# Wb's last four row tiles: 32x32 blocks from the load and a VectorE transpose, in place of TensorE transposes

## The reference

```
x = x + ffn0(cond0(x))     x = x + ffn1(cond1(x))
cond0: x W0^T + 2 * sum over the top-2 of 8 experts of gate * B0 (A0 x), gates from x Wr0 and a bias per language id
ffn0:  top-1 of 8 experts by logits, logit * Bw (A x)
cond1: x W1^T + b1 + 2 * (x As[slot]) Bs[slot], slot per batch element
ffn1:  x Wb^T + b_base + 2 * sum over the top-2 of 8 experts of weight * B1 (A1 x)
```

## Time and profile before

| | |
|---|---|
| median of three runs | 500.59 us |
| the profiled execution, device time | 501.62 us |
| its span, first to last instruction | 499.6 us |
| mean granted TensorE clock | 0.989 |
| TensorE busy / VectorE / ScalarE | 98% / 54% / 27% of the span |

### The profile page before, as it was taken

The page is one execution under the profiler, slowest core; times in us unless marked ns, Lnnn a source line. Parts: engine busy times, 40 slices in busy tenths (PEclk is TensorE's granted clock), DMA queues, the critical chain, the costliest instruction groups (busy, mean ns, idle before and its releaser), DMA issues.

```text
span 499.6 us, 8465 instructions
## 1 busy us (share of the span) xinstructions
PE 487.5 (98%) x3007; PEld 466.5 (93%) x3007; DVE 267.6 (54%) x825; ACT 135.9 (27%) x300; POOL 9.5 (2%) x18
## 2 busy tenths in 40 slices
PE   6999999999999988999999999999999999999997
PEld 4988899999999878999999999999999999999997
DVE  3745864544446746475465574656557457445211
ACT  4444630111111331232132232132124123212111
POOL 2040000000000000000000000000000000000000
PEclk9987999999999999999999999999999999999999
DMA  8975525221111145107304312611710910200111
GB/s 258 331 253 178 183 72 139 106 63 43 42 42 48 44 62 78 54 4 120 71 5 95 53 46 64 83 42 60 89 42 2 148 44 2 64 31 16 59 42 43
DMA packets 86621, 40.22 MB, mean 81 GB/s; under 512 B 68503, under 2 KB 80545, under 8 KB 86462
## 3 DMA queue, kind: packets, MB, share of 16 engines
q1 hardware_dynamic: 86318, 39.25, 31.3%
q0 software_dynamic: 272, 0.56, 0.5%
HBM read 28.64 MB, written 11.16 MB: 80 GB/s over the span
## 4 chain that ended last, share of the span: by engine, by line
PE 96%; DVE 2%; DMA 1%; ACT 1%; issue 0%; DVEq 0%; ACTq 0%
PE banks L1054 28%; PE banks L1056 28%; PE banks L1055 28%; PE banks L1049 5%; PE banks L1068 3%; PE banks L1239 2%; PE banks L1103 1%; DMA a0f<-in_L_ffn_A_dram 1%; PE banks L1077 0%; PE banks L1201 0%; PE banks L1244 0%; DVE xTlo L705 0%; DVE x_raw L752 0%; PE banks L1249 0%; DVE a0f L741 0%
## 5 line engine op out<-in xcount | busy, mean ns | idle before, releaser
L1054 PE MATMUL banks<-Mhi,x1Thi 128*128 128x392 f32 x384 | 137.0, 357 | 2.0 <-DVE x1Tlo L705 1.5
L1055 PE MATMUL banks<-Mlo,x1Thi 128*128 128x392 f32 x384 | 130.6, 340 | 0.0
L1056 PE MATMUL banks<-Mhi,x1Tlo 128*128 128x392 f32 x384 | 130.5, 340 | 0.0
L1054 PEld LDWEIGHTS banks<-Mhi,x1Thi 128*128 128x128 f32 x384 | 72.3, 188 | 4.5 <-issue 2.4
L1054 PE MATMUL banks<-WbThi,ws_hi 128*128 128x392 f32 (+2 forms) x216 | 74.7, 346 | 0.0
L1056 PE MATMUL banks<-WbThi,ws_lo 128*128 128x392 f32 (+2 forms) x216 | 73.2, 339 | 0.0
L1055 PE MATMUL banks<-WbTlo,ws_hi 128*128 128x392 f32 (+2 forms) x216 | 73.0, 338 | 0.0
L1055 PEld LDWEIGHTS banks<-Mlo,x1Thi 128*128 128x128 f32 x384 | 72.5, 189 | 0.0
L1056 PEld LDWEIGHTS banks<-Mhi,x1Tlo 128*128 128x128 f32 x384 | 72.2, 188 | 0.0
L1056 PEld LDWEIGHTS banks<-WbThi,ws_lo 128*128 128x128 f32 x216 | 40.7, 188 | 3.2
L1055 PEld LDWEIGHTS banks<-WbTlo,ws_hi 128*128 128x128 f32 x216 | 40.6, 188 | 3.1
(11 more groups left out here) (180 smaller groups left out, 772.8 us busy)
## 6 DMA issues: line engine op xcount, KB each, us to landing
wraw<-in_L_cond_W_dram SPq DMA_DIRECT2D x16, 512.0 KB, 3.9
out_dram<-ybuf SPq DMA_DIRECT2D x15, 512.0 KB, 3.1
x_raw<-in_x_dram SPq DMA_DIRECT2D x56, 128.0 KB, 3.9
wraw<-in_L_ffn_W_base_dram SPq DMA_DIRECT2D x8, 512.0 KB, 6.5
xin_first<-in_x_dram SPq DMA_DIRECT2D x1, 1024.0 KB, 9.5
x1T_dram<-xin_first SPq DMA_DIRECT2D x1, 1024.0 KB, 3.9
wraw<-x1T_dram SPq DMA_DIRECT2D x2, 512.0 KB, 3.5
Fbuf<-fe_hi_dram SPq DMA_DIRECT2D x16, 64.0 KB
```

Of the source, the lines that this page charges most:

```text
L1054: pe.matmul(out_, l[0], r[0], start=start, stop=False, **kw)
L1055: pe.matmul(out_, l[0], r[1], start=False, stop=False, **kw)
L1056: return pe.matmul(out_, l[1], r[0], start=False, stop=stop, **kw)
```

## The change

Wb tiles 0 to 3 are handled as before. Tiles 4 to 7 are loaded by `load_blocks`, four DMAs each, turned in place by one VectorE transpose (`turn_wb`), and split by one ScalarE copy and one VectorE subtraction of 128x1024 (`wb_part` on both) straight from the `wraw` buffer. Their eight units go. New semaphores: `wb_in` (a tile has landed), `wb_turned_in` (VectorE has turned it), `wb_hi`, `wb_lo` (its parts are there). ScalarE's and VectorE's orders are rewritten, TensorE's fe steps stand alone, and TensorE waits for wb_lo 2 before fe step 8 and for wb_lo 4 before fe step 16. The W1 loads wait for `wb_lo` in place of the units. The counts that wait for W1's and later loads fall by one load for each buffer.

```diff
@@ SyncE
-                sp.dma_start(wraw[o % 4][:, :], Wb[o * P:(o + 1) * P, :]).then_inc(wraw_in[o % 4], 16)
+                if o < 4:
+                    sp.dma_start(wraw[o][:, :], Wb[o * P:(o + 1) * P, :]).then_inc(wraw_in[o], 16)
+                else:
+                    load_blocks(wraw[o - 4], Wb, o, wb_in[o - 4])
...
             for n in range(4):
-                sp.wait_ge(unit_done, wb_turned(4 + n))
+                sp.wait_ge(wb_lo, n + 1)
                 load_w1(n, n)
@@ helper
+        def wb_parts(o):
+            raw = wraw[o - 4][:, :].rearrange("p (k c) -> p k c", k=K)
+            return [(raw, [t[:, :, RC + o * P:RC + (o + 1) * P] for t in (WbThi, WbTlo)])]
@@ ScalarE
-            copy_units(NEF, units_second[NEF - NU1:NEF - NU1 + 4])
+            def wb_part(o):
+                act.wait_ge(wb_turned_in, o - 3)
+                for raw, (hi, _) in wb_parts(o):
+                    ins = act.activation(hi, raw, ACT.Copy)
+                ins.then_inc(wb_hi, 1)
+
+            copy_units(NEF, units_second[NEF - NU1:NEF - NU1 + 2])
+            wb_part(4)
             hgT_part(0)
-            copy_units(NEF + 4, units_second[NEF - NU1 + 4:NEF - NU1 + 8])
+            wb_part(5)
             keep_fe(0)
-            copy_units(NEF + 8, units_second[NEF - NU1 + 8:NEF - NU1 + 10])
+            wb_part(6)
+            wb_part(7)
             xT_part(1, 1, xT_first, XT_FIRST[1])
             whT_part(0, 0)
-            copy_units(NEF + 10, units_bw)
+            copy_units(NEF + 2, units_bw)
@@ VectorE
-            lo_units(NEF, units_second[NEF - NU1:NEF - NU1 + 4])
+            def turn_wb(o):
+                dve.wait_ge(wb_in[o - 4], 64)
+                tile = wraw[o - 4][:, :]
+                dve.transpose(tile, tile).then_inc(wb_turned_in, 1)
+
+            def wb_part(o):
+                dve.wait_ge(wb_hi, o - 3)
+                for raw, (hi, low) in wb_parts(o):
+                    ins = lo(low, raw, hi)
+                ins.then_inc(wb_lo, 1)
+
+            lo_units(NEF, units_second[NEF - NU1:NEF - NU1 + 2])
+            turn_wb(4)
             hgT_part(0)
-            lo_units(NEF + 4, units_second[NEF - NU1 + 4:NEF - NU1 + 8])
+            turn_wb(5)
+            wb_part(4)
             keep_fe(0)
             top1(0)
-            lo_units(NEF + 8, units_second[NEF - NU1 + 8:NEF - NU1 + 10])
+            turn_wb(6)
+            wb_part(5)
+            turn_wb(7)
+            wb_part(6)
+            wb_part(7)
             xT_part(1, 1, xT_first, XT_FIRST[1])
             whT_part(0, 0)
-            lo_units(NEF + 10, units_bw)
+            lo_units(NEF + 2, units_bw)
@@ TensorE
-            for n, unit in enumerate(units_second[NEF - NU1:NEF - NU1 + 10]):
-                if n == 4:
-                    turn_small(hg_ready, 1, pt_hg, hg[:, :], thg_done)
-                if n == 8:
-                    add_lora0(0)
+            for n, unit in enumerate(units_second[NEF - NU1:NEF - NU1 + 2]):
                 turn_units(NEF + n, [unit])
-                if n == 8:
-                    pe.wait_ge(unit_lo, wb_turned(5))
                 fe_steps(n, n + 1)
+            fe_steps(2, 6)
+            turn_small(hg_ready, 1, pt_hg, hg[:, :], thg_done)
+            fe_steps(6, 8)
+            add_lora0(0)
+            pe.wait_ge(wb_lo, 2)
+            fe_steps(8, 10)
             pe.wait_ge(fe_lo, 1)
             turn_x(xin_first[:, D:2 * D], XT_FIRST[1])
             turn_small(wh_ready, 1, pt_wh, wh[:, :], twh_done)
-            turn_units(NEF + 10, units_bw)
+            turn_units(NEF + 2, units_bw)
             fe_steps(10, 12)
             small0(1, 1, xT_first)
             fe_steps(12, 2 * K)
             pe.wait_ge(unit_lo, NU2)
+            pe.wait_ge(wb_lo, 4)
             fe_steps(2 * K, 18)
```

More of the change, by code:

```diff
@@ L161, in adaln_ffn @@
         w1_hi, w1_lo = sem("w1_hi"), sem("w1_lo")
+        wb_in, wb_turned_in = [sem(f"wb_in{i}") for i in range(4)], sem("wb_turned_in")
+        wb_hi, wb_lo = sem("wb_hi"), sem("wb_lo")
         m_done, m_hi, m_lo = sem("m_done"), sem("m_hi"), sem("m_lo")
@@ L223, in adaln_ffn @@
         units_bw = turn_b(bw_j, BwThi, BwTlo, 1.0, [(bw_j_ready, 1)])
-        units_b1 = turn_b(wraw[2], B1Thi, B1Tlo, 2.0, [(wraw_in[2], 16 * 8)])
+        units_b1 = turn_b(wraw[2], B1Thi, B1Tlo, 2.0, [(wraw_in[2], 16 * 7)])
         units_wb = []
-        for o in range(K):
+        for o in range(4):
             for k0 in (0, 4):
@@ L286, in half_tiles, with block_rows @@
             return t[:, :].rearrange("p (k c) -> p k c", k=K)[:, 4 * h:4 * h + 4, half * P:(half + 1) * P]
-        def block_rows(t):
-            return xf[bass.ds(t * P, P), :].rearrange("(i r) (k j c) -> j r k i c", r=BLK, j=NJ, c=BLK)
+        def block_rows(src, t):
+            return src[bass.ds(t * P, P), :].rearrange("(i r) (k j c) -> j r k i c", r=BLK, j=NJ, c=BLK)
         def raw_tile(raw, half, h=None):
@@ L312, in _, with load_blocks @@
             w0v = W0.rearrange("(p j) i -> p j i", j=K)
-            def load_blocks(tile, t, s):
-                src = block_rows(t)
+            def load_blocks(tile, rows_of, t, s):
+                src = block_rows(rows_of, t)
                 for j in range(NJ):
@@ L370, in _ @@
             sp.wait_ge(fe_stored, 32)
-            load_blocks(x_raw1[:, 0:D], 2, x2_in)
+            load_blocks(x_raw1[:, 0:D], xf, 2, x2_in)
             sp.wait_ge(acc_step, 1)
@@ L401, in load_x @@
             def load_x(t, half, raw):
-                load_blocks(raw[:, half * D:(half + 1) * D], t, x_in[half])
+                load_blocks(raw[:, half * D:(half + 1) * D], xf, t, x_in[half])
             sp.wait_ge(w1_hi, K - 1)
@@ L594, in _ @@
             exp0(0)
-            copy_units(NEF, units_second[NEF - NU1:NEF - NU1 + 4])
+            def wb_part(o):
[5 more added lines that the diff above has]
+            wb_part(4)
             hgT_part(0)
-            copy_units(NEF + 4, units_second[NEF - NU1 + 4:NEF - NU1 + 8])
+            wb_part(5)
             keep_fe(0)
-            copy_units(NEF + 8, units_second[NEF - NU1 + 8:NEF - NU1 + 10])
+            wb_part(6)
+            wb_part(7)
             xT_part(1, 1, xT_first, XT_FIRST[1])
             whT_part(0, 0)
-            copy_units(NEF + 10, units_bw)
+            copy_units(NEF + 2, units_bw)
             exp0(1)
-            act.wait_ge(wraw_in[0], 80)
+            act.wait_ge(wraw_in[0], 64)
             act.activation(ws_hi[0][:, :], wraw[0][:, :], ACT.Copy).then_inc(w1_hi, 1)
@@ L608, in _ @@
             keep_fe(2)
-            act.wait_ge(wraw_in[1], 80)
+            act.wait_ge(wraw_in[1], 64)
             act.activation(ws_hi[1][:, :], wraw[1][:, :], ACT.Copy).then_inc(w1_hi, 1)
@@ L629, in _ @@
                     keep_m(i, par)
-                    act.wait_ge(wraw_in[2 + par], i * 16 + 16 * 5)
+                    act.wait_ge(wraw_in[2 + par], i * 16 + 16 * 4)
                     act.activation(ws_hi[par][:, :], wraw[2 + par][:, :], ACT.Copy).then_inc(w1_hi, 1)
@@ L646, in _ @@
                 if g == 0:
-                    act.wait_ge(wraw_in[2], 16 * 9)
-                    act.wait_ge(wraw_in[3], 16 * 8)
+                    act.wait_ge(wraw_in[2], 16 * 8)
+                    act.wait_ge(wraw_in[3], 16 * 7)
                 x1T_part(0, 0, g, sums(g))
```

## The result

The changed kernel takes 507.13 us, the median of six runs (505.29 to 512.26), against 501.12 us, the median of six of the kernel before (500.29 to 504.64). The ratio over all these runs is 1.0129, with a 95% interval of 1.0070 to 1.0188; the two medians alone give 1.0120, which lies inside it. The forecast was 506.9 us, slower. The execution that was profiled after is a long one, 511.0 us on the device, of which the span is 509.2 us; so stretches are compared here, and not whole spans.

The account below looks back on a forecast made before the run. TensorE, holding 96% of the chain of waits, was taken as the bound. A 4.3 us later small0 plus 2.0 us of lowered clock made 6.3 us, taking the median from 500.59 to 506.9 us, range 504.2 to 509.0.

Parts of the forecast that it names:

- The bound: TensorE holds 96% of the chain of waits, with no later slack to swallow a delay made in the changed stretch.
- What is removed: Eight units of transposes on TensorE, 3.5 us, and a 0.40 us wait: 3.9 us of path if nothing else is late.
- The first wait: TensorE before add_lora0(0), waiting 1.5 us for hgT_lo because ScalarE copies tile 4 ahead of its hgT half.
- The second wait: TensorE before fe step 8, idle 6.8 us for wb_lo 2, as tile 5's subtraction follows tile 6's transpose on VectorE.
- The shift of small0: Second small0 starts 4.3 us later, at 68.58 and not 64.31, and the shift lasts to the kernel's end.
- the bounds 2.5 to 5.2: Limits in us on the 4.3 us shift: VectorE's chain without two idle stretches, or every hand-over at 0.14 us.
- The clock: TensorE's clock falls to 1.2 GHz through the 6.8 us idle, costing 1.0 to 2.7 us behind it, 2.0 taken.
- the slow stretch: Low-clock time behind the idle, taken as 2.1 to 5.5 us like earlier rows; at most half of it lost.
- The loads: Block DMAs of tiles 4 to 7 cost nothing; tile 5 has 5 us to spare and more.
- Sum: Whole kernel: 4.3 us of shift plus 2.0 us of clock, 6.3 us slower, median 506.9 us.
- The clock that holds: Rival: the same wait at TensorE but no fall of the clock, 504.9 us; chance 14%.
- The rival on the other side: Rival: tiles come in time, wb_lo 2 by 57.1, and TensorE keeps its 3.9 us, 496.7 us; chance 4%.

Follow-up runs that it names:

- e4: Changed kernel, VectorE and ScalarE reordered: tiles 4 and 5 turned before the first gates, last two subtractions behind the Bw units; 499.60 us, ratio 0.9976 to before.
- e6: e4 with the subtractions of tiles 6 and 7 moved from VectorE to GpSimd; 498.72 us, ratio 0.9965 to the kernel before.
- e2: Changed kernel with twelve dead fe steps (36 matmuls) on TensorE between add_lora0 and the wait for wb_lo 2; 505.20 us, ratio 1.0082 to before.
- e1: Changed kernel run again with no edit; 507.05 us, ratio 1.0125 to the kernel before.
- e5: Changed kernel with VectorE's subtraction of tile 5 moved ahead of keep_fe(0), top1(0) and the transpose of tile 6; 505.02 us, ratio 1.0072 to before.
- e10: e6 repeated with no edit; 499.38 us, ratio 0.9988 to the kernel before.
- e12: e6 with VectorE's transpose of tile 5 moved behind the first gates; 499.63 us, ratio 0.9970 to the kernel before.
- e3: Changed kernel with tiles 4 to 7 loaded by one DMA each in 4 KB rows, output wrong; 507.61 us, ratio 1.0130 to before.
- e8: Kernel before with only the block loads of tiles 4 to 7 added, TensorE's transposes kept, output wrong; 501.04 us, ratio 0.9996 to before.
- e7: Half the change: only tiles 6 and 7 in blocks on VectorE, 4 and 5 left to TensorE's transposes; 501.21 us, ratio 1.0005 to before.
- e9: e6 with tile 4's subtraction on GpSimd too, three in all; 501.91 us, ratio 1.0032 to the kernel before.
- e11: e6 with tiles 4 to 7 loaded by one DMA each in 4 KB rows, output wrong; 498.46 us, ratio 0.9954 to before.

## Why the prediction was right, step by step

- **The bound.** That TensorE has no slack behind the stretch held: 435.2 us from small0 to the end after, 435.3 before.
- **What is removed.** 3.9 us. e4 and e6 get 2.45 and 3.2 us of it, with 1.1 and 0.6 us of waiting left in the stretch: together 3.6 and 3.8.
- **The first wait.** 1.5 us for hgTlo was forecast, 1.25 measured, for the reason named: ScalarE's copy of tile 4 ahead of hgT, VectorE idle 1.29 us (1.4 forecast).
- **The second wait.** 6.8 us was forecast, 6.47 measured; the subtraction of tile 5 ends 13.89 us after brow (63.80 - 49.76 = 14.04 forecast), directly behind the transpose of tile 6. The small difference is the subtraction, 1.18 us and not 1.22, and shorter hand-overs.
- **The shift of small0.** 4.3 us forecast, 4.15 measured, in e2, where the clock plays no part. Of the terms this is the one on which the sum rests, and the bounds 2.5 to 5.2 were needed for nothing.
- **The clock.** 2.0 us was taken of 1.0 to 2.7; the traces show 2.1 and 2.4, the medians 1.85. That the clock would fall was argued and held. Its size is in part luck. The prediction took the length of the slow stretch, 2.1 to 5.5 us, from the earlier trace rows, but those are the lengths for which the rows were asked, and not how long the clock was low. The microseconds in which it changes, in the trace of before (same columns):

```profile
34.00:35.00 1.00, 1.00 (x5) 0.67 (x4) 0.34 (x2) 0.51 (x1) 0.00 (x0) 0.60 0.16 44
...
41.00:42.00 1.00, 1.00 (x6) 0.63 (x5) 0.84 (x2) 0.55 (x1) 0.00 (x0) 0.99 0.99 291
...
44.00:45.00 1.00, 1.00 (x7) 0.94 (x7) 0.87 (x2) 0.40 (x1) 0.00 (x0) 0.72 0.64 262
...
47.00:48.00 1.00, 1.00 (x7) 1.00 (x6) 0.24 (x1) 0.00 (x0) 0.00 (x0) 0.58 0.00 0
```

By them it was low from 34.2 to 41.0 and from 44.4 to 47.8, 6.8 and 3.4 us, with TensorE busy throughout, and not "thinly used". The prediction also let the slow stretch begin behind the idle. In fact the clock is low for 10.2 us (56.9 to 67.15 in e1), from within the idle on; the 4.5 and 5.0 us of it that fall on work happen to lie between 2.1 and 5.5. The sentence of the Trainium skill that stands beside this term in the prediction (TensorE: Matmul & The Clock Gate, section Loop structure matters more than you think) agrees with these traces: the granted clock fell to 0.50 in the idles of 6.5 us (after and e1), and e2, without the idle, kept 1.00. It is less plain where the idle comes in parts: the clock fell in e5, with 1.28 and 2.95 us, and in e10, with 0.56, 1.13 and 0.58 us; it stayed at 1.00 in e4, with 0.53 and 0.58 us, and in e12, with 1.18 and 0.58 us.
- **The loads.** Cost at nothing, and so they did: e3 and e8. The prediction's estimate of 5 us to spare for tile 5 is for the changed order, where it is wanted 6.8 us after brow (59.94 in the first trace). e10 shows the other side: where the transpose of tile 5 is wanted some 8 us earlier, the loads are the next bound.
- **Sum.** 6.3 us forecast; 6.27 and 6.52 us in the two traces; by the ratios 1.0129 and 1.0125 of 500.6 us, 6.5 and 6.3 us.
- **The rivals.** The clock that holds, 504.9 us, is e2's result: 505.20. It was the right price for the wrong case. The rival on the other side, 496.7 us, needed wb_lo 2 by the time TensorE gets there; with the order of this change it is 6.5 us late, and e6 shows that with another order, and two subtractions on GpSimd, it is 0.6 us late; even so the gain by the ratios is 1.8 us (e6) and 0.6 us (e10), and not 3.9. The argument against it counted VectorE's 6.0 us of work from 52.6 as if none of it could be done earlier. That is right for the change as made, and it isn't a limit of the idea.

One thing the prediction didn't foresee, and it didn't need it: the profiled execution after took 3.4 us longer to brow than that of before. The clock was at 0.59 and 0.50 from 44 to 50 us, and TensorE had waited 0.9 us for the routers at 42. The same wait, 0.6 to 1.2 us, is in e1, e3, e7, e9, e10 and e12, and not in before, e2, e4, e6, e8 and e11. That it is in e3, with plain loads, and not in e4 and e6, with block loads, speaks against the block loads as its cause. Brow lay between 48.04 and 53.15 over all the traces, with and without that wait. What sets it was not tried; I take it for spread of the executions; single profiled spans can't be compared to better than that.

## What to carry to other kernels

Work that is moved off the bounding engine is paid for in the other engines' queues: before counting the gain, walk the in-order list of the engine that takes it over, and look at what now stands ahead of the one result that the bounding engine wants next. Here the same instructions cost 6.3 us in one order and gained 1.2 us in another (e4). And an idle of the bounding engine that is long enough to lower its clock costs more than its length, here 6.5 us of idle and 2.1 to 2.4 us more behind it; measure the two apart by filling the idle with dead matmuls.

## What the runs showed of the hardware

- The granted clock fell to 0.50, the 1.2 GHz level, within idles of 6.5 us (after, e1), and stayed low for 10.2 us. It fell in e5 too, 0.6 us behind idles of 1.28 and 2.95 us that had 0.6 us of matmuls between them, and in e10 at 56.7, in the last of three idles of 0.56, 1.13 and 0.58 us between 52.7 and 56.9; there it was low for 3.4 us each. With idles of 1.18 and 0.58 us (e12) and of 0.53 and 0.58 us (e4) it stayed at 1.00. In before it was low from 34.2 to 41.0 us with no idle of TensorE.
- VectorE turns the 32x32 blocks of 128x1024 of f32 in 1.23 to 1.25 us. GpSimd takes 2.4 us to subtract 128x1024 of f32, VectorE 1.2 us; in e6 GpSimd's two subtractions (61.1 to 65.9) ran beside VectorE's work, and TensorE had no wait in that time.
- While the blocks of tiles 4 to 6 came in, four DMAs of 128 KB in 128-byte runs for each tile, all of the core's DMA together moved 125 to 145 GB/s (42 to 48 us, after). The kernel before, with whole rows of 4 KB, moved 285 to 311 GB/s from 38 to 44 us and next to nothing from 46 to 48. Tile 5's blocks were there by 48.5 to 49.7 us in e4, e6, e9 and e10.
- VectorE stopped for 5.2 us, with nothing shown that it waited for, at the second turn of the loop in e9 alone, and the trace of e9 alone has 18 packets on q14, against 12 to 14.
